# Token weights in the gathered rows, paired gathers and an earlier tile 7 in a routed feed-forward kernel

## The reference

```python
base = einsum('bsi,oi->bso', x, W_base)
h = einsum('bsi,ji->bsj', x, Wt)
z = einsum('bsj,brj->bsr', h, A[idx]);  l = einsum('bsr,bor->bso', z, B_w[idx])
y = base + einsum('bso,po->bsp', l, Wp) * scaling[idx][:, None, None]

probs = softmax(y @ gate_w.T)                      # 2048 tokens x 16 experts
topk_w, topk_idx = top_k(probs, 2)
topk_w = topk_w / (sum(topk_w, -1, keepdims=True) + 1e-20)
g, u = y @ w_gate[e].T, y @ w_up[e].T              # 512 -> 352, for every expert e
out = x + sum over a token's two experts e of  topk_w[e] * ((silu(g) * u) @ w_down[e].T)
```

## Time and profile before

| What | Value |
|---|---|
| time, median of 3 runs | 345.91 us (345.72 to 346.19) |
| time of the profiled execution | 347.69 us |
| its span | 345.9 us |
| mean granted TensorE clock | 0.999 |
| PE busy | 336.5 us (97%) |
| PEld busy | 296.8 us (86%) |
| DVE busy | 235.1 us (68%) |
| ACT busy | 178.8 us (52%) |
| POOL busy | 124.4 us (36%) |
| DMA | 82.49 MB, mean 238 GB/s |

### The profile page before, as it was taken

How to read it: one execution, slowest core, us unless ns; L and a number is a source line. 1 busy time by engine, 2 the same in 40 slices (tenths; PEclk the granted TensorE clock), 3 DMA queues, 4 the chain that set the end, 5 groups by cost and what they waited for, 6 DMA issues and landing times.

```text
span 345.9 us, 7808 instructions
## 1 busy us (share of the span) xinstructions
PE 336.5 (97%) x1875; PEld 296.8 (86%) x1875; DVE 235.1 (68%) x308; ACT 178.8 (52%) x242; POOL 124.4 (36%) x85
## 2 busy tenths in 40 slices
PE   8999999999999899999999999999999999999993
PEld 4677778788899799999899999999999998989992
DVE  0576699988464658485878866797758588779410
ACT  1479722522545464655567554755545675575222
POOL 0000000022354452536276544647326271354233
PEclk9999999999999999999999999999999999999999
DMA  7990992946599789998989999699999969932144
GB/s 278 389 488 33 340 342 76 352 143 206 193 293 332 186 212 323 204 326 212 310 206 306 330 321 248 152 305 296 285 314 251 282 187 287 303 59 34 7 65 63
DMA packets 47928, 82.49 MB, mean 238 GB/s; under 512 B 5552, under 2 KB 22576, under 8 KB 47792
## 3 DMA queue, kind: packets, MB, share of 16 engines
q1 hardware_dynamic: 38912, 62.96, 55.6%
q0 software_dynamic: 8960, 18.89, 24.7%
HBM read 60.59 MB, written 19.92 MB: 233 GB/s over the span
## 4 chain that ended last, share of the span: by engine, by line
PE 85%; DMA 7%; DVE 2%; issue 2%; SPq 1%; DVEq 1%; POOLq 0%; ACT 0%; POOL 0%; ACTq 0%
PE bank L693 39%; PE bank L722 21%; PE bank L449 5%; PE bank L549 4%; PE bank L553 4%; PE bank L550 4%; PE bank L667 4%; DMA w_raw<-wall 4%; DMA xs<-xg 2%; DMA xg<-y_rows,gidx 1%; PE bank L465 1%; PE bank L480 1%; PE bank L610 1%; PE bank L576 1%; SPq L428 1%
## 5 line engine op out<-in xcount | busy, mean ns | idle before, releaser
L1250 POOL DMA_INDIRECT out<-ys,sidx x40 | 75.3, 1882 | 123.1 <-DMA out<-ys,sidx 69.7
L355 DVE TENSOR_TENSOR w_lo<-w_raw,w_hi (+2 forms) x32 | 76.4, 2386 | 10.6 <-issue 8.4
L1229 POOL DMA_INDIRECT xg<-y_rows,gidx x40 | 48.6, 1216 | 95.6 <-issue 79.8
L693 PE MATMUL bank<-w_hi,xt_hi 128*128 x320 | 82.0, 333 | 0.2 <-issue 0.2
L693 PE MATMUL bank<-w_hi,xt_lo 128*128 x320 | 79.0, 323 | 0.0
L693 PE MATMUL bank<-w_lo,xt_hi 128*128 x320 | 79.0, 323 | 0.0
L353 ACT ACTIVATE w_hi<-w_raw (+2 forms) x32 | 64.7, 2021 | 8.0 <-DMA w_raw<-wall 4.4
L847 ACT ACTIVATE sg<-bank 128x352 f32<-128x352 f32 x40 | 18.4, 461 | 76.4 <-PE bank L693 70.1
L693 PEld LDWEIGHTS bank<-w_lo,xt_hi 128*128 128x128 f32 x320 | 56.1, 189 | 0.0
L693 PEld LDWEIGHTS bank<-w_hi,xt_lo 128*128 128x128 f32 x320 | 56.1, 189 | 0.0
L693 PEld LDWEIGHTS bank<-w_hi,xt_hi 128*128 128x128 f32 x320 | 54.6, 189 | 1.4 <-issue 0.8
(11 more groups left out here) (181 smaller groups left out, 364.1 us busy)
## 6 DMA issues: line engine op xcount, KB each, us to landing
w_raw<-wall SPq DMA_DIRECT2D x16, 1408.0 KB
w_raw<-wall SPq DMA_DIRECT2D x16, 768.0 KB
xs<-xg SPq DMA_DIRECT2D x132, 64.0 KB
x_st<-xin SPq DMA_DIRECT2D x8, 512.0 KB, 12.0
y_rows<-y_st SPq DMA_DIRECT2D x16, 256.0 KB, 4.1
head_sb<-head SPq DMA_DIRECT2D x2, 640.0 KB, 5.1
wb_sb<-wb SPq DMA_DIRECT2D x2, 512.0 KB, 8.9
wbt_sb<-wbt SPq DMA_DIRECT2D x2, 512.0 KB, 10.5
```

The source lines that it names most:

```text
L355: e.tensor_tensor(w_lo[:, bass.ds(dst, n)], raw, hi, ALU.subtract).then_inc(own, 1)
L693: mm = e.matmul(bank[2 + 2 * s + t % 2][:, 0:INTER], a, w[:, bass.ds(at + (k * GU + s * INTER), INTER)], start=k == 0 and i == 0, stop=k = ...
L1229: e.indirect_dma_start(out=xg[t % NXG][:], out_offset=None, in_=y_dram, in_offset=bass.IndirectOffsetOnAxis(ap=gidx[:, t:t + 1], axis=0)). ...
L1250: e.indirect_dma_start(out=out, out_offset=bass.IndirectOffsetOnAxis(ap=sidx[:, t:t + 1], axis=0), in_=ys[t % NYS][:], in_offset=None, bou ...
```

## The change

The token weights no longer pass through the slot tables. A row of `y_dram` and of `xg` is now 528 floats wide: 512 of y, then 16 of which two are the token's two weights. VectorE makes both weights for all tokens in `token_weights` (six small operations), from `e_two`, the exponential of the second-highest logit less the highest, which ScalarE computes in one more small activation. One DMA on SyncE's queue, at c = 11 and ahead of the store of chunk 11, writes `w12` beside the rows: 2048 pieces of 64 bytes. Gather 0 waits for it (`d_row`). A new `weigh(t, ...)` on VectorE picks, for each tile, the first or the second weight of the gathered row (`is_top` says which) into `wtab`.

So `slot_tables` is called once, the columns 2 to 4 of `oh_q`, the three operations on `wtab` and the bf16 parts of the weights go. The index tables change with it: column 0 holds the chunk, column 1 the place plus 1 (plus 128 for the second choice).

The orders change too: `x_turn(0)` stands one k-step earlier; `h_turn(0)` goes into the middle of `gate_up(1)`; the gathers go 2 and 3 together, then (after `x_turn(2)`) 4 and 5, then (after `h_turn(1)`) 6, then 7 before scatter 0, 8 and 9 before scatter 1. The second load's `dn` waits until gather 2 has landed. `rows_apart(7)` comes ahead of `later_weights(3)`. On ScalarE tile 3's gu split goes behind `x_evac(2)`, and on VectorE at t = 2 `y_low(3)` and `h_low(1)` go ahead of tile 3's gu split. The split of ScalarE no longer waits for the second table.

```diff
-TABS = 5
+TABS, YW, W_PAD = 3, H + 16, 16
-AT_TURN, AT_RANKS, AT_TABLES, AT_NEED, AT_X = (3, 3), (6, 0), (12, 1), (12, 3), (CH - 1, 2)
+AT_TURN, AT_RANKS, AT_TABLES, AT_NEED, AT_X = (3, 3), (6, 0), (12, 1), (12, 3), (CH - 1, 1)
-N_LEAD, N_COPY, N_SOON = 9, 5, 4
+N_LEAD, N_COPY, N_SOON = 9, 4, 3
-N_EARLY, C_FLOOR, N_AHEAD = 2, 12, 5
-C_SECOND, N_LATE = CH - 1, 3
+N_EARLY, C_FLOOR, N_AHEAD = 2, 12, 7
+C_ROW, N_LATE = 11, 3
...
-        y_dram = nc.dram_tensor("y_rows", [NTOK, H], F32, kind="Internal").ap()
+        y_dram = nc.dram_tensor("y_rows", [NTOK, YW], F32, kind="Internal").ap()
...
                     if t < NSPLIT:
-                        e.wait_ge(m_tb, 2)
+                        e.wait_ge(m_y, CH)
...
+                if c == C_ROW:
+                    e.wait_ge(v_w12, 2)
+                    e.dma_start(y_dram.rearrange("(c p) w -> p c w", p=P)[:, :, H:YW], w12[:]).then_inc(d_row, 16)
                 e.wait_ge(a_y, c + 1)
-                e.dma_start(y_dram[c * P:(c + 1) * P, :], y_st[c % NYST][:]).then_inc(d_y[c % NYST], 16)
-                if c == C_SECOND:
-                    e.wait_ge(v_w12, 1)
-                    for part in PARTS:
-                        e.wait_ge(d_w[part], 16)
-                        load_part(e, part, table(e, T_REX, 1, 0, NEXP - 1), 0)
+                e.dma_start(y_dram[c * P:(c + 1) * P, 0:H], y_st[c % NYST][:]).then_inc(d_y[c % NYST], 16)
...
+            for part in PARTS:
+                e.wait_ge(d_w[part], 16)
+                load_part(e, part, table(e, T_REX, 1, 0, NEXP - 1), 0)
+                e.wait_ge(d_g[N_EARLY], 16)
...
-                        if t == 2 and k == KH // 2:
+                        if t in (1, 2) and k == KH // 2:
                             h_turn(t - 1)
...
             gate_up(0)
-            e.wait_ge(v_ohq, 1)
-            e.wait_ge(v_need, 1)
-            slot_tables(bank[7], 2, TABS - 2)
-            words[1] = tile_word(e, 1)
-            h_turn(0)
             gate_up(1)
...
             y_stage(3)
+            e.wait_ge(v_cho, 1)
+            e.activation(e_two[:], cc[2][:], ACT.Exp).then_inc(a_exp, 1)
             e.activation(first_silu[:], cs[:, C_ID:C_ID + 1], ACT.Silu)
...
-                    if t == 0:
-                        e.wait_ge(v_w, 1)
+                    e.wait_ge(*weighed(t))
...
-            split_weights(e, count, 3, ahead, "gu", a_gu)
             silu(1)
             x_evac(2)
+            split_weights(e, count, 3, ahead, "gu", a_gu)
...
+            def token_weights():
+                e.wait_ge(a_exp, 2)
+                step(e.tensor_reduce(sums[:], ex[:], AX_X, ALU.add))
+                step(e.reciprocal(w_one[:], sums[:]))
+                step(e.tensor_tensor(w_two[:], e_two[:], w_one[:], ALU.mult))
+                step(e.scalar_tensor_tensor(w_sum[:], w_one[:], 1e-20, w_two[:], ALU.add, ALU.add))
+                step(e.reciprocal(w_inv[:], w_sum[:]))
+                e.tensor_tensor(w12[:, :, 0], w_one[:], w_inv[:], ALU.mult).then_inc(v_w12, 1)
+                e.tensor_tensor(w12[:, :, 1], w_two[:], w_inv[:], ALU.mult).then_inc(v_w12, 1)
...
+            def weigh(t, done_by):
+                row = xg[t % NXG]
+                e.wait_ge(d_g[t % NXG], 16 * (t // NXG + 1))
+                e.scalar_tensor_tensor(wtab[:, t:t + 1], row[:, H:H + 1], is_top[:, t:t + 1], row[:, H + 1:H + 2],
+                                       ALU.mult, ALU.max).then_inc(done_by, 1)
+
             def x_turned(t):
                 n = t - N_PE
                 with in_use(e, count, t):
+                    weigh(t, v_wx)
...
             y_low(0)
-            weigh(1)
-            e.wait_ge(v_chain, done[0])
-            e.tensor_tensor(where, where, wide(w_part[2][:]), ALU.mult).then_inc(v_ohq, 1)
+            weigh(0, v_wt)
...
                     if t == 2:
-                        split_weights(e, count, t + 1, word, "gu", v_gu)
+                        y_low(t + 1)
+                        weigh(t + 1, v_wt)
                     if t <= NFULL:
                         h_low(t - 1)
-                    if t + 1 < N_PE:
+                    if t == 2:
+                        split_weights(e, count, t + 1, word, "gu", v_gu)
+                    if 3 <= t < N_PE - 1:
                         y_low(t + 1)
+                        weigh(t + 1, v_wt)
...
+                if t == 0:
+                    e.wait_ge(d_row, 16)
                 e.sem_inc(p_turn, 1)
                 gather(t)
             for i in range(NYST):
                 e.wait_ge(d_y[i], 16 * (CH // NYST))
             gather(2)
-            e.wait_ge(m_ht, 1)
             gather(3)
             e.wait_ge(m_xt, 3)
             gather(4)
+            gather(5)
+            e.wait_ge(m_ht, 2)
+            gather(6)
```

101 lines of the change are left out of this document (39 added, 62 removed).

## The result

| What | Before | Changed |
|---|---|---|
| median | 345.88 us (345.06 to 346.92, 22 runs) | 348.87 us (345.34 to 352.51, 22 runs) |
| ratio of the times | | 1.0071, 95% interval 1.0050 to 1.0091 |
| profiled execution, its span | 347.69, 345.9 us | 348.83, 346.9 us |
| TensorE busy | 336.5 us | 335.4 us |
| GpSimd busy | 124.4 us | 135.9 us |

The forecast was 344.2 and faster. The kernel is 0.7% slower, and its runs lie further apart: 7 us from the fastest to the slowest, where before has 2 on the same chip. The two profiled executions are not alike either. Before's was 1.8 us over its median, after's stands at its median.

What follows compares the result with a forecast made beforehand. TensorE's own list of work was taken as the bound, busy 336.5 of 345.9 us. Terms -2.0 - 0.3 + 1.2 - 1.4 + 0.2 + 0.6 = -1.7 us gave 344.2 us from 345.91; range 342.7 to 347.2.

Steps and rivals of the forecast that it cites:

- Second slot table: TensorE between the two gate_up: 32 matmuls of the second table go, all 2.0 us won.
- Gather 2: Gather 2 asked for 2.0 us earlier, TensorE's 0.3 us wait goes; if still held to its old landing, costs 2.0.
- Tile 3's split: Before h_turn(2): product(2) stands behind the reordered gu split on VectorE, so TensorE waits 1.2 us; bounds 0.5 to 1.8.
- One weighing per tile: VectorE's 40 added 0.22 us operations: cost 0.2 us at product(4), covered elsewhere.
- Row copy: At x_turn(0): 64-byte pieces at 27 ns delay gather 0 by 3.5 us, less 2.8 slack: cost 0.6 us.
- Tile 7's copies: Before down(4): copies issued ahead of the fourth load remove all but 0.15 of a 1.55 us wait, gain 1.4.
- the dear row copy: Rival: small pieces read before written cost 54 ns each, gather 0 wait 4.1 us, total 347.7; chance 0.18.
- the copies don't help: Rival: the wait before down(4) stays as VectorE's wait for the dn split, total 345.6; chance 0.07.

Runs made afterwards that it cites:

- e9: Kernel before without its second slot table, every slot's weight 0.5, orders unchanged: 346.63 us, ratio 1.0014.
- e6: Kernel before with token weights in the rows, the two turns that go with them and tile 3's split moved; gathers, loads, copies ordered as before: 347.62 us, ratio 1.0010.
- e18: Changed kernel with VectorE's old order at t = 2 for tile 3's split: 350.34 us, ratio to before 1.0139.
- e3: Kernel before with rows of 2112 bytes, the gap filled from x by one early DMA and not used: 347.98 us, ratio 1.0017.
- e12: Kernel before with half of the bytes of each load from the third on: 345.70 us, ratio 0.9988.
- e13: Kernel before, unchanged, one execution for a second trace: 346.65 us, span 344.8.
- the pair with light loads: Changed kernel and kernel before, each with half of the bytes of every load from the third on (e11, e12): 345.43 and 345.70 us.
- e1: Changed kernel with each load from the fourth on asked for one tile later, behind one more tile's copies: 352.31 us, ratio to before 1.0163.
- e2: Kernel before with only the change's values of SyncE's order (N_COPY 4, N_SOON 3): 351.75 us, ratio 1.0118.
- e4: Changed kernel with fewer gathers ahead of scatter 0 (N_AHEAD 5; gather 5 before scatter 0, 6 and 7 before scatter 1): 349.19 us, ratio to before 1.0035.
- e5: Changed kernel with SyncE's old order (N_COPY 5, N_SOON 4): 352.87 us, ratio to before 1.0117.
- e10: Kernel before with only the paired gathers and the second load in two steps: 347.02 us, ratio 1.0010.
- e14: Kernel before with the copies of tiles 7 and 8 ahead of the fourth load (N_SOON 3, N_COPY still 5): 352.96 us, ratio 1.0195.
- e7: e6 with tile 3's split back at its old place on ScalarE and VectorE: 347.34 us, ratio to before 0.9989.
- e15: e7 with the second load in two steps, its dn waiting for gather 2: 346.09 us, ratio to before 1.0005.
- e17: e15 with ScalarE's new order and VectorE's old one for tile 3's split: 346.53 us, ratio to before 1.0030.
- S: Part of the change: SyncE's new order of loads and copies (N_COPY 4, N_SOON 3); alone on the kernel before (e2) 351.75 us, ratio 1.0118.
- e8: Changed kernel again, unchanged, beside later runs: 349.52 us, ratio to before 1.0032.
- e11: Changed kernel with half of the bytes of each load from the third on: 345.43 us, ratio to before 0.9997.
- G: Part of the change: gathers in pairs with the second load in two steps; alone on the kernel before (e10) 347.02 us, ratio 1.0010.

## Why the prediction was wrong

Step by step, in the order of the forecast:

- **Second slot table, -2.0: right at its place.** `h_turn(1)` starts 1.9 us earlier: the table's 2.0 and gather 2's 0.3, less 0.5 for gather 0, make 1.8 of it. "I take all 2.0" held in the changed order of TensorE. In e9, which takes the table out and changes no order, 1.2 of it is lost at `h_turn(0)`.
- **Gather 2, -0.3: right, but by luck in its margin.** I had it land near 86 and be asked for at 88.4. It starts at 83.61, lands 5.2 us later, at 88.8, and TensorE takes it at 88.86, without a wait and with nothing to spare. e6 shows the other outcome that I had named: with before's order the lead is lost to a wait of 1.2 us.
- **Tile 3's split, +1.2: right, 0.94.** VectorE's `product(2)` started at 98.90, directly behind the split of 95.89.
- **One weighing per tile, +0.2: nothing to see.** Between `h_turn(3)` and `h_turn(4)` the balance stays at -0.7.
- **Row copy, +0.6: the size is right, 0.5, by two errors that cancel.** A piece took 14 ns of the queue's time (10 of a DMA engine's), not 27, so the copy held store 11 up by 1.8 us and not 3.5. But store 11's data ended near 71.0 and gather 0 started at 73.05, 2 us later, where I had taken 1.1. The Trainium skill, "DMA: Bandwidth & Descriptors", Specifications, states a read-modify-write below 512 bytes; the price of 54 ns, twice 27, that my rival set on that was my own estimate. The trace does not agree with that price; whether a piece is read before it is written, no run here shows.
- **Tile 7's copies, -1.4: wrong, in two ways.** The wait before `down(4)` did go. But it came back one tile further, at 0.7 us (1.7 in e18), since tile 8's copies now stood behind the fourth load. And it was not typical of before: the second trace does not have it, and those of e3 and e12, which leave the orders of before as they are, have 0.27 and none. I had noted that the profiled execution took 1.8 us more than the median, and used that only to shift the sum. The table under e13 shows that this one wait puts the first trace 1.7 us behind the second; e13 loses some of this again later (0.62 at 190 us among it).

Up to 128.7 us the sum was -1.7 and the trace has -1.4. That agreement is luck in part, since both are counted from the one trace of before that had the wait. Without the term for the copies the sum is -0.3; the traces have -0.7 to -1.1 at `h_turn(4)`, and the pair with light loads (345.43 against 345.70) agrees with -0.3 but cannot tell it from 0. So the step that was mis-sized is the -1.4 for the copies, and the step that gives the sign is this one: "After that the other engines keep ahead of TensorE, but for small waits of a few tenths, and I look for the change's effect between 65 and 121 us." Behind 121 us the DMA engines are busy for 96% of the time, and SyncE's and GpSimd's queues hold copies, loads, gathers and scatters that wait for one another. The change moved the fourth load behind tile 7's copies, every later load one tile forward, ahead of copies that before had gone first, and each scatter behind more gathers. I costed what these moves bring at their first use and nothing of what they do over the 33 tiles that follow. There the two traces of the changed kernel show late `xs` twice each, with waits of TensorE of 0.7 to 1.3 us, 2.0 and 2.1 in all; e1, e2, e4, e5, e10 and e14 have one of 2.3 to 6.6 us behind a late `xs` or `w_raw`. The changed kernel is about 3 us slower in the median. e6, e7, e15 and e17, which keep before's order on SyncE and GpSimd (e15 and e17 but for dn of the second load), have none over 0.5 us there.

The rival that ended slower, the dear row copy, was wrong too; its sign was right for another reason. The one that came nearest in its mechanism, though not in its time, was that the copies don't help, at 345.6.

The traces side by side say something of which part makes which wait. Of the five traces with S and full loads, four have a wait before `down(5)`, for tile 8's rows, whose copies S puts behind the fourth load: 0.69 (changed), 1.72 (e18), 3.64 (e2) and 6.59 us (e4); e8 has none. No trace with another order on SyncE has one there, nor has S with light loads (e11). And e1, e5 and e10, which have G and ask for the loads from the fifth on where before did, have their longest waits behind late weights, at 237.39, 238.64 and 195.09.

What stays open: how G and S act together. Alone, S costs 1.2% (e14, which sets the fourth load behind the copies of tiles 7 and 8 and moves nothing else, 2.0%) and G nothing that can be told, G with the weights in the rows and the split's new place 1.2%, and both with these 0.3 to 0.7%. So they seem to make up for each other in part; that early gathers spare S's copies their wait is argued, not shown. The waits behind tile 8's stand elsewhere in each execution, and no experiment followed one of them through all queues. The tail is open as well. From the last scatter's issue to the end it took 3.8 to 4.1 us in the seven traces with the second table, 4.5 to 4.9 in the ten with the weights in the rows and full loads, 4.1 and 4.3 in the two of those with light loads, and 5.1 in e9. So it takes some 0.7 us of what the changed kernel could win, at a place that the forecast put at nothing, and I did not find why.

## What to carry to other kernels

- A term that rests on one wait in one trace is worth what the median says of that execution. Where the profiled run is over the median by about that wait, take a second trace before the wait is counted as gain.
- When an edit reorders a queue that is used in every tile, cost it in the stretch where the DMA engines are full, not at the tile for which it was made. Halving the bytes in both kernels is the quick test of whether a loss is the order's alone or needs the full loads.
- TensorE's work is also cover. Ahead of taking 2 us from it, list what the other engines do beneath them. Here some 1 us of a split came into the open, and every order of it moved the wait and did not remove it.
